# A fused two-layer ViT tower: strip copy and key masking moved from GpSimd to ScalarE, with new instruction orders on five engines

## The reference, cut to what matters

```python
h = patchify(x) @ W.T + b;  h = concat(cls_tok, h)          # 17 tokens x 192
h = h + topk_softmax_attention(layernorm(h))                # 12 heads of 64, 12 of 17 keys kept
h = h + ternary_gated_ffn(layernorm(h))                     # 8-bit activations, weights -1, 0, 1
h = h + linear_attention(layernorm(h))                      # below
h = h + norm_ffn(layernorm(h))                              # 192 -> 128 -> 192 -> layer norm

# in linear_attention, causal over the 17 tokens of an image:
q_f = elu(q) + 1;  k_f = elu(k) + 1                         # 12 heads of 16
params = silu(x @ Wb1) @ Wb2;  gate = f(tanh(params))
out = norm(sum_j (q_f.k_f[j]) * (1 + gate[j]) * v[j] / (sum_j q_f.k_f[j]))
```

## Time and profile before

| | |
|---|---|
| median of three runs | 668.53 us |
| profiled execution, its own time | 664.79 us |
| its span on the core | 662.9 us |
| PE busy | 577.5 us, 87% of the span |
| DVE busy | 501.5 us, 76% |
| POOL busy | 352.9 us, 53% |
| ACT busy | 254.9 us, 38% |

### The profile page before, as it was taken

One profiled execution on the slowest core, in us unless ns is written; L12 is line 12 of the kernel. 1 busy time (PEld: TensorE's weight loads), 2 busy tenths in 40 slices (PEclk: granted clock), 3 DMA queues, 4 the chain that ended last, 5 costly groups with the idle time before them and its releaser, 6 DMA issues.

```text
span 662.9 us, 15406 instructions
## 1 busy us (share of the span) xinstructions
PE 577.5 (87%) x5065; PEld 471.7 (71%) x5065; DVE 501.5 (76%) x2149; ACT 254.9 (38%) x659; POOL 352.9 (53%) x884
## 2 busy tenths in 40 slices
PE   4467889999999999999999999999999999787553
PEld 3255567878878787877878787787878878665441
DVE  0527558798898989889898988989898898875532
ACT  2014233544535354453535445353544535232210
POOL 2011023666666666666666666666666656555542
PEclk9679989999999999999999999999999999867575
DMA  9730010000100100010000000000000000000000
GB/s 212 162 81 1 1 43 22 2 22 1 28 19 11 28 1 28 3 26 13 13 26 0 26 0 26 13 13 26 0 6 0 7 2 8 6 1 7 0 7 7
DMA packets 11122, 14.92 MB, mean 23 GB/s; under 512 B 2161, under 2 KB 8658, under 8 KB 11078
## 3 DMA queue, kind: packets, MB, share of 16 engines
q1 hardware_dynamic: 8774, 12.69, 7.6%
q10 hardware_dynamic: 2304, 1.67, 0.9%
HBM read 12.68 MB, written 1.67 MB: 22 GB/s over the span
## 4 chain that ended last, share of the span: by engine, by line
PE 60%; DVE 23%; issue 4%; SPq 4%; ACT 3%; POOL 3%; DMA 1%; DVEq 0%; POOLq 0%; ACTq 0%
PE bank_embed L1210 8%; PE bank_att L1284 6%; PE bank_lin L1368 5%; PE bank_embed L1180 5%; PE bank_embed L1215 5%; DVE kept L718 5%; PE bank_att L1086 4%; PE bank_att L1274 4%; SPq L387 3%; DVE scores L698 3%; PE bank_lin L1384 3%; DVE top L710 2%; PE bank_att L1244 2%; PE bank_ffn L1086 2%; PE bank_lin L1086 2%
## 5 line engine op out<-in xcount | busy, mean ns | idle before, releaser
L1210 PE MATMUL bank_embed<-norm0T,w_qkv 128*128 128x119 f32 x456 | 59.4, 282 | 8.5 <-DMA g_out<-L_ffn_g_out 6.8
L1210 PEld LDWEIGHTS bank_embed<-norm0T,w_qkv 128*128 128x128 f32 x456 | 56.8, 197 | 11.2 <-issue 6.8
L483 POOL TENSOR_TENSOR rstd<-spread,minus_half 119x1 f32<-119x1 f32 (+1 forms) x95 | 57.3, 603 | 7.5
L482 POOL TENSOR_TENSOR spread<-moments,gain_eps 119x1 f32<-119x1 f32 x57 | 12.2, 214 | 85.2 <-DVE moments L673 85.1
L742 DVE TENSOR_TENSOR weightsT<-bank_lin,consts 119x476 f32<-119x476 f32 x57 | 36.8, 648 | 18.3 <-PE bank_lin L1368 18.3
L984 ACT COPY qkT<-bank_embed 128x357 f32<-128x357 f32 x76 | 30.9, 462 | 42.6 <-PE bank_embed L1215 42.6
L698 DVE TENSOR_REDUCE scores<-bank_att 119x51 f32<-119x357 f32 x76 | 37.6, 517 | 12.3 <-PE bank_att L1244 11.0
L1368 PE MATMUL bank_lin<-feat_qk,feat_k 32*119 32x119 f32 x456 | 42.5, 277 | 3.0 <-DVE weightsT L742 2.6
L483 POOL TENSOR_TENSOR rstd_h<-spread_h,minus_half 119x12 f32<-119x12 f32 x19 | 43.3, 2277 | 1.5
L950 ACT COPY att1T<-bank_lin 96x238 f32<-96x238 f32 x19 | 6.7, 353 | 94.2 <-PE bank_lin L1086 94.2
L1180 PE MATMUL bank_embed<-w_tok,patchT 128*119 128x192 f32 x228 | 42.3, 337 | 0.6 <-ACT patchT L960 0.6
(11 more groups left out here) (232 smaller groups left out, 1551.8 us busy)
## 6 DMA issues: line engine op xcount, KB each, us to landing
strips<-x SPq DMA_DIRECT2D x19, 336.0 KB
out<-result ACTq DMA_DIRECT2D x18, 89.2 KB
w_qkv<-L_attn_w_qkv SPq DMA_DIRECT2D x2, 576.0 KB, 8.4
w_in_raw<-L_ffn_w_in SPq DMA_DIRECT2D x1, 768.0 KB, 12.4
w_tok_raw<-L_tok_W SPq DMA_DIRECT2D x1, 576.0 KB
w_qkv_rest<-L_attn_w_qkv SPq DMA_DIRECT2D x2, 288.0 KB, 9.2
w_o<-L_attn_w_out SPq DMA_DIRECT2D x1, 576.0 KB
w_qkv_raw<-L_attn_Wqkv SPq DMA_DIRECT2D x1, 432.0 KB
```

The lines of the kernel that those rows point to most:

```text
L483: pool.tensor_tensor(rstd_out, spread, minus_half[0:ROWS, 0:spread.shape[1]], ALU.pow) \
L1210: pe.matmul(parts((E0, E1)[s], 3)[:, j], w_qkv0[:, tile * 128:(tile + 1) * 128], norm0T[:, s, :], start=j == 0, stop=False, skip_group_che ...
```

## The change

Two steps move from POOL to ACT. `p_strips` becomes `a_strips`, one ACT copy with the same patterns; a small padding operation of POOL that stood ahead of the copy is dropped. `p_feat_k` becomes `a_feat_k`, two ACT activations (Copy) with the 0/1 column as their per-partition scale. What waits for them, and for what they wait, is unchanged.

The order lists of POOL, DVE, ACT and PE are all rewritten. Some steps are also moved across the end of the iteration: `t_qk(0)` and `t_norm3` from the start of an iteration to the end of the one before, and so for `v_norm3`, `v_probs`, `v_hidT`, `p_rstd3`, `p_gate` and `a_tanh_par`; their stage number falls by one with it, so that they still work on the same group.

```diff
--- before.py
+++ after.py
@@ -483,14 +483,6 @@
                 pool.tensor_tensor(rstd_out, spread, minus_half[0:ROWS, 0:spread.shape[1]], ALU.pow) \
                     .then_inc(rstd_ready, 1)
 
-            def p_strips(g, p):
-
-                pool.wait_ge(strips_in[p], 16 * (g // 2 + 1) if isinstance(g, int) else 8 * (g - p) + 16)
-                after(pool, S["patches1"], g)
-                pool.tensor_tensor(pad_pool[:, :], pad_pool[:, :], ones[:, 0:1], ALU.mult)
-                pool.tensor_copy(patches[:, :, :].rearrange("p x (r c) -> p x r c", r=PATCH),
-                                 strips[:, p].rearrange("p r (x c) -> p x r c", x=GRID)).then_inc(S["strips_cut"], 1)
-
             def p_rstd0(g, p):
                 pool.wait_ge(S["moments0"], g + 1)
                 rstd(g, chain_of(pool, S["spread0"], 1), S["rstd0"], moments0[:, 1:2], spread0[:, :], rstd0[:, :], eps_ln)
@@ -521,14 +513,6 @@
                 pool.wait_ge(S["moments2"], g + 1)
                 norms_chain(g, pool.tensor_tensor(spread2[:, 0], moments2[:, 1:2].to_broadcast([ROWS, 2]), gain2, ALU.mult))
                 rstd(g, norms_chain, S["rstd2"], spread2[:, 0], spread2[:, 1], rstd2[:, :], eps2)
-
-            def p_feat_k(g, p):
-
-                pool.wait_ge(S["feat_k_all"], g + 1)
-                for odd in range(2):
-                    keep = consts[0:HALF, C_PARITY + odd:C_PARITY + odd + 1].unsqueeze(2).to_broadcast([HALF, 2, ROWS])
-                    last = pool.tensor_tensor(feat_k[:, odd], feat_qk[:, 2:4, :], keep, ALU.mult)
-                last.then_inc(S["feat_k"], 1)
 
             def p_gate(g, p):
 
@@ -571,8 +555,8 @@
                 rstd(g, last_chain, S["rstd4"], moments4[:, 1:2], spread4[:, :], rstd4[:, :], eps_ln)
 
             iterations(pool, lambda i, parity, active: in_turn(i, parity, active, [
-                (1, p_h0), (0, p_strips), (5, p_h3_beta), (5, p_rstd3), (4, p_feat_k), (4, p_gate), (3, p_scaled), (3, p_rms),
-                (5, p_rstd4), (4, p_centred_sq), (4, p_rstd_h), (3, p_rstd2), (0, p_rstd0), (2, p_rstd1),
+                (3, p_scaled), (3, p_rms), (5, p_h3_beta), (5, p_rstd4), (1, p_h0), (4, p_centred_sq), (4, p_rstd_h),
+                (3, p_rstd2), (0, p_rstd0), (4, p_rstd3), (2, p_rstd1), (3, p_gate),
             ]), setup)
 
 
@@ -900,12 +884,11 @@
                 ((S["a_done01"], S["a_masked0"], L1), (S["a_done01"], S["a_masked1"], L0), (S["a_done2"], S["a_masked2"], L1)))]
 
             iterations(dve, lambda i, parity, active: in_turn(i, parity, active, [
-                (5, v_norm3), (4, v_feat), (4, v_hidT), (3, v_big_in), (2, v_probs), (2, v_wide(0)), (2, v_wide(1)),
-                (5, v_stats4), (4, v_causal[0]), (2, v_wide(2)), (3, v_gated), (4, v_causal[1]), (4, v_causal[2]), (4, v_v1),
-                (3, v_big_out), (4, v_ratio), (5, v_result), (2, v_h1), (4, v_sq_sum), (2, v_u_in), (1, v_pack(1, A1)),
-                (3, v_h2), (3, v_stats2), (1, v_pack(0, A0)), (4, v_att1), (0, v_h0), (0, v_stats0), (3, v_norms2),
-                (1, v_pack(3, A1)), (1, v_pack(2, A0)), (0, v_norm0), (1, v_top), (4, v_h3), (1, v_drop), (4, v_stats3),
-                (1, v_mix),
+                (2, v_wide(0)), (4, v_feat), (2, v_wide(1)), (3, v_big_in), (2, v_wide(2)), (5, v_stats4), (4, v_causal[0]),
+                (4, v_causal[1]), (3, v_gated), (4, v_causal[2]), (4, v_v1), (3, v_big_out), (4, v_ratio), (2, v_h1),
+                (4, v_sq_sum), (2, v_u_in), (3, v_h2), (1, v_pack(0, A0)), (3, v_stats2), (1, v_pack(1, A1)), (4, v_att1),
+                (0, v_h0), (0, v_stats0), (3, v_norms2), (1, v_pack(3, A1)), (0, v_norm0), (1, v_pack(2, A0)), (5, v_result),
+                (1, v_top), (1, v_drop), (4, v_h3), (1, v_mix), (4, v_stats3), (1, v_probs), (4, v_norm3), (3, v_hidT),
             ]), setup)
 
 
@@ -950,6 +933,13 @@
                     act.copy(dst, src).then_inc(done_sem, 1)
                 return step
 
+
+            def a_strips(g, p):
+
+                act.wait_ge(strips_in[p], 16 * (g // 2 + 1) if isinstance(g, int) else 8 * (g - p) + 16)
+                after(act, S["patches1"], g)
+                act.copy(patches[:, :, :].rearrange("p x (r c) -> p x r c", r=PATCH),
+                         strips[:, p].rearrange("p r (x c) -> p x r c", x=GRID)).then_inc(S["strips_cut"], 1)
 
             def a_patchT(n, bank_tile, turned, done_sem):
 
@@ -1031,6 +1021,14 @@
                 act.activation(exp_qk[:, :, :], parts(L1, 4)[0:HALF], ACT.Exp)
                 act.activation(relu_qk[:, :, :], parts(L1, 4)[0:HALF], ACT.Relu).then_inc(S["relu_qk"], 1)
 
+            def a_feat_k(g, p):
+
+                act.wait_ge(S["feat_k_all"], g + 1)
+                for odd in range(2):
+                    last = act.activation(feat_k[:, odd], feat_qk[:, 2:4, :], ACT.Copy,
+                                          scale=consts[0:HALF, C_PARITY + odd:C_PARITY + odd + 1])
+                last.then_inc(S["feat_k"], 1)
+
             def a_tanh_hid(g, p):
                 act.wait_ge(S["hid"], g + 1)
                 act.activation(tanh_hid[:, :], L0[:, 0:ROWS], ACT.Tanh, scale=0.5)
@@ -1068,11 +1066,12 @@
                     act.dma_start(out[bass.ds(g * ROWS, ROWS), :], result[:, p]).then_inc(stored[p], 16)
 
             iterations(act, lambda i, parity, active: in_turn(i, parity, active, [
-                (4, a_tanh_par), (3, a_int_in), (5, a_hid1), (1, a_qk(0)), (3, a_in_T), (2, a_probsT[1]), (2, a_probsT[0]),
-                (3, a_tanh_gate), (1, a_qk(1)), (2, a_probsT[2]), (3, a_square), (4, a_interference), (4, a_num_T),
-                (2, a_att[0]), (0, a_patchT(0, E0, S["patches0"], S["patchT0"])), (2, a_att[1]), (3, a_int_out), (3, a_out_T),
-                (0, a_patchT(1, E1, S["patches1"], S["patchT1"])), (4, a_att1_T), (3, a_norms_T), (0, a_norm0T), (3, a_qk1),
-                (0, a_v(1)), (0, a_v(0)), (3, a_tanh_hid), (5, a_store), (4, a_norm3_T), (1, a_exp),
+                (4, a_feat_k), (5, a_hid1), (3, a_int_in), (2, a_probsT[0]), (3, a_in_T), (1, a_qk(0)), (2, a_probsT[2]),
+                (2, a_probsT[1]), (3, a_tanh_gate), (0, a_strips), (3, a_square), (4, a_interference), (1, a_qk(1)),
+                (2, a_att[0]), (4, a_num_T), (0, a_patchT(0, E0, S["patches0"], S["patchT0"])), (2, a_att[1]), (3, a_int_out),
+                (0, a_patchT(1, E1, S["patches1"], S["patchT1"])), (3, a_out_T), (4, a_att1_T), (3, a_norms_T), (0, a_norm0T),
+                (3, a_qk1), (0, a_v(1)), (0, a_v(0)), (1, a_exp), (3, a_tanh_hid), (4, a_norm3_T), (3, a_tanh_par),
+                (5, a_store),
             ]), setup)
 
             act.wait_ge(stored[0], 16 * ((GROUPS + 1) // 2))
@@ -1432,12 +1431,12 @@
                 pe.matmul(M1[0:ROWS, 0:EMBED], hid1T[:, :], w2o[:, :], start=True, stop=True).then_inc(S["out4"], 1)
 
             iterations(pe, lambda i, parity, active: in_turn(i, parity, active, [
-                (5, t_norm3), (1, t_qk(0)), (4, t_params), (5, t_hid1), (4, t_lin((0, 1), S["a_done01"])), (3, t_int_in),
-                (5, t_out4), (2, t_probs(0)), (2, t_probs(1)), (3, t_gate), (1, t_qk(1)), (2, t_probs(2)),
-                (4, t_lin((2,), S["a_done2"])), (2, t_att0(1)), (2, t_att0(0)), (4, t_num),
-                (0, t_patches(0, E0, S["k_copied0"], S["patches0"])), (4, t_num_turn), (2, t_proj0), (3, t_int_out),
-                (0, t_patches(1, E1, S["k_copied1"], S["patches1"])), (1, t_dots(0)), (3, t_down), (0, t_embed),
-                (1, t_dots(1)), (4, t_att1), (3, t_norms2), (4, t_proj1), (0, t_norm0), (3, t_qk1), (0, t_v), (3, t_hid),
+                (4, t_params), (2, t_probs(0)), (5, t_hid1), (4, t_lin((0, 1), S["a_done01"])), (5, t_out4), (3, t_int_in),
+                (2, t_probs(1)), (2, t_probs(2)), (3, t_gate), (1, t_qk(1)), (4, t_lin((2,), S["a_done2"])), (2, t_att0(1)),
+                (2, t_att0(0)), (4, t_num), (0, t_patches(0, E0, S["k_copied0"], S["patches0"])), (4, t_num_turn),
+                (2, t_proj0), (0, t_patches(1, E1, S["k_copied1"], S["patches1"])), (3, t_int_out), (1, t_dots(0)),
+                (3, t_down), (0, t_embed), (1, t_dots(1)), (4, t_att1), (3, t_norms2), (4, t_proj1), (0, t_norm0), (3, t_qk1),
+                (0, t_v), (3, t_hid), (0, t_qk(0)), (4, t_norm3),
             ]), setup)
 
 
```

## The result

The changed kernel takes 674.38 us (median of 8 runs, 669.69 to 676.06) against 668.50 for the kernel before in the same series (8 runs, 664.18 to 673.75). The ratio is 1.0105, 95% interval 1.0072 to 1.0138: slower by 1%. The profiled execution took 676.06, its span is 674.2.

What follows compares the result with a forecast made beforehand. PE was taken to bound the kernel. Filling -5.3, steady part +7.6 and draining 0 summed to +2.3 us on 668.53, giving 670.8 us; the range was 662 to 677.5.

Steps and rivals of the forecast that it cites:

- the steady part: Entries into iterations 5 to 19: +0.43 us per ordinary iteration, +0.72 at a branch, together +7.6 us.
- uncovered: At a loop branch, PE's own branch stands between `t_norm3` and `t_params` with nothing hiding it: +0.57 us.
- gain 0.20: PE's wait before `norm3` goes, as `t_norm3` stands behind `t_qk(0)`: 0.20 us gained in an ordinary iteration, 0.63 at a branch.
- The filling: Start of the kernel, through iteration 4: early `t_qk(0)` gains, later waits give some back; sum -5.3 us (-6.7 to -2.4).
- The first term: Filling: first group's `t_qk(0)` runs ahead of the setup wait, in PE's old gap; -5.0 us, taken as -4.2 for the clock.
- a wait of 0.86 goes twice: -1.7: Filling, iterations 2 and 3: `t_probs(2)` ahead of `t_qk(1)` removes a 0.86 us wait before the attention, -1.7 us in all.
- The draining: Last iterations, where PE waits for chains (hidT, the gate, the head norm): costed at 0, 1.5 us either way.
- the third: Rival: the filling gives nothing because DVE's setup or the next setup steps' DMAs set its end; 675 us, chance 0.14.
- The first: Rival, faster: the two new waits don't come about, the store not holding ACT up; 664.0 us, chance 0.30.
- The second: Rival, slower: ACT's queue becomes the path from `t_params` to `t_lin`, with a wait of 0.85; 677 us, chance 0.16.
- The fourth: Rival: the strips copy on ACT delays `a_square` by 0.3 us per iteration; 675 us, chance 0.04.
- The rule of the ports: POOL and DVE share a port pair, so 2.25 us less POOL per group could bring DVE's end of the iteration forward.

Runs made afterwards that it cites:

- the kernel without gaps: Changed kernel with DVE's h3 ahead of the drop step, ACT's store ahead of the copies of v, and `t_probs(1)` ahead of `t_lin`: ratio 0.9929 to before.
- the transposes together: Changed kernel with ACT's store ahead of the copies of v and DVE's h3 ahead of the drop step, `t_probs(1)` and `t_probs(2)` adjacent: ratio 0.9969 to before.
- the moves alone: Kernel before with its own order lists, only the key masking and the strips copy moved from POOL to ACT: 665.59 us, ratio 0.9965 to before.
- the kernel with the late order: Changed kernel with `t_qk(0)` of the first three groups put back behind the setup steps: ratio 1.0123 to before.
- store early: Changed kernel with the store's DMA issue on ACT ahead of the copies of v: 665.55 us, ratio 0.9987 to before.
- the orders alone: Changed kernel with its new order lists, but key masking and strips back on POOL: 690.39 us, ratio 1.0339 to before.

## Why the prediction was right or wrong

**The mechanism of the steady part was right: the places of the gaps and their sum. The conversion into time was wrong.** By its own terms the prediction gives for the 13 periods measured here (9 ordinary, 4 at a branch) gaps of 8.7 us before `t_lin`, 2.3 before `t_hid` and -4.3 before `norm3`, together +6.7. The rows say 9.0, 2.1 and -4.6: +6.5. Two errors inside cancel: the ordinary gap was 0.59 in the loop, not 0.45, since the store holds ACT up until 0.32 after its issue starts; that at the branch was 0.91, not 1.17, since PE's own branch, put at 0.57 "uncovered", shows no cost, while ACT's, put at 0.15, shows 0.32. Yet the steady part grew by 2.5 us, not 6.5: 4.0 us less. PE's start-to-start times in one ordinary iteration, 531.29 on in before and 536.64 on in after, show why: from `t_hid` to `t_num` without the gap PE takes 13.33 in before and 12.99 in after, for the same steps. The largest piece is at the end of `t_hid`, in before and in after:

```profile
547.28 0.60 PE L1338 MATMUL bank_lin<-norms2T,w_g 96*128 96x119 f32 x4
548.09 0.41 PE L1086 MATMUL bank_ffn<-consts,norm 119*96 119x119 f32 x2 [0.21 <-DVE norm L876]
```

```profile
552.83 0.60 PE L1337 MATMUL bank_lin<-norms2T,w_g 96*128 96x119 f32 x4
553.26 1.50 PE L1209 MATMUL bank_embed<-norm0T,w_qkv 128*128 128x119 f32 x12
```

Its last four matmuls take 0.81 - 0.21 = 0.60 net of the gap where `t_norm3` waited behind them, and 0.43 where `t_qk(0)` follows at once. **The failing step is "gain 0.20" for the norm3 wait: removing it gave back the gap and 0.17 more, the end of the last matmuls, which the next step now overlaps.** By "TensorE: Matmul & The Clock Gate" of the Trainium skill (section "Single matmul latency") a single bf16 matmul at the full clock takes about 0.166 us beyond its columns; the 0.17 of these float32 rows is of that size. Over 13 iterations the 0.17 makes 2.2 of the 4.0 us. The rest lies in smaller pieces of either sign, which the prediction took as unchanged. The new waits have such a price as well: without its gap of 0.14 it is 0.91 from the start of the matmuls ahead of `t_hid` to its own, against 0.83 in before, and for `t_lin` 0.69 against 0.59. All pieces together show in PE's busy time: cut from `t_num` to `t_num`, an ordinary iteration of the loop has 28.32 of 28.77 us in before (299.63 on) and 27.94 of 29.04 in after (303.30 on). The period of 28.57 us of the kernel without gaps against 28.58 of before without its gap, and 28.28 with the transposes together, shows that which step follows which is worth 0.3 us per iteration. Why the transposes pay 0.3 for being split stays open.

**Strips and masks.** 1.07 against 1.05 and 0.88 against 0.86 predicted. Both were worked out from neighbours of like shape, and with the moves alone the steady part shows no cost.

**The filling** was put at -5.3. The first term is right: over the eight profiles of after and its variants with the early `t_qk(0)` and both steps on ACT, `t_embed` of iteration 1 starts at 45.1 on average (43.6 to 46.6), over the three with the late one at 49.2 (47.7 to 50.0), 4.2 less. **The failing step is the second, "a wait of 0.86 goes twice: -1.7".** In iteration 3 that wait went, but `wide` (1.53) and `int_in` (0.99) came, with a lower clock, and iteration 3 became 3.5 us longer than in the kernel with the late order. At `t_num` of iteration 4 the same eight and three are at 128.7 (125.2 to 130.7) and 129.7 (125.8 to 132.2): -1, within their scatter.

**The draining** was put at 0, with 1.5 either way, by the waits alone. **That is the largest miss: +6 to +9 us. Of these 5.5 to 6.2 lie in the two iterations in which the clock was lower, and go when it is held; the rest was not tested.** The prediction had weighed the clock in the filling, for one step, and nowhere else.

**The sum**: 2.5 - 1 and 6 or more is 7.5 or more between profiles, where the medians are 5.9 apart (a profile is one execution, and the filling and draining scatter); the forecast was 7.6 - 5.3 + 0 = 2.3. That the range held is in part luck: the steady part was put 4 us too high, the filling 4 too low and the draining 6 to 9 too low. Of the rivals, the third (675) named the time, for its reason only in part: the filling gave little, but the setup was not what took it back. The first was right about the store: with its hold-up gone (store early) the wait is 0.22, where it had 0.2, and the ratio is 0.9987, not to be told from 1. The second, ACT's queue as the path, is where the wait is, but at 0.6 and not 0.85. The fourth did not come. The point forecast lay within 0.5% of before; slower, which had 0.37, is what came.

**The rule of the ports.** With POOL's copy and masks gone DVE's busy time in an iteration of the loop, ordinary and at a branch, is 25.57 and 25.64, against 25.31 and 25.40 in before with the same cuts: nothing was given back. In before they held up no long operation of DVE: the first mask started behind `feat_qk`, overlapped it by 0.23 us (316.76 to 316.99) and itself took 0.68, where the second took 0.58; and `h3`, beside which the copy ran, has only one of its inputs in SBUF. In the orders alone POOL and DVE held each other up. "SBUF — State Buffer" of the Trainium skill (section "SBUF: two separate sides") has the engine that starts first hold the port pair for its whole instruction, and the other blocked. The rows of the orders alone agree: `rstd` (329.05) ends 0.39 after the `wide` that had started before it (329.68), `wide` (330.23) 0.51 after the first mask (330.75), and the second mask (331.69) 0.43 after that `wide` (331.26), each 0.14 to 0.16 less than it takes alone (0.55, 0.65 and 0.58). So each waited for the other's end with all but its first 0.15 us. Such a wait is in after, too, which shows both cases:

```profile
321.61 0.65 DVE L736 TENSOR_TENSOR wide<-probs,consts 119x476 f32<-119x476 f32 x1
321.63 1.02 POOL L483 TENSOR_TENSOR rstd<-spread,minus_half 119x1 f32<-119x1 f32 x1
...
350.68 0.54 POOL L483 TENSOR_TENSOR rstd<-spread,minus_half 119x1 f32<-119x1 f32 x1
350.80 0.66 DVE L736 TENSOR_TENSOR wide<-probs,consts 119x476 f32<-119x476 f32 x1
```

Where `wide` starts first, `rstd` takes 1.02 in place of 0.54. Where `rstd`, one number per partition, starts first, `wide` is not held up, though they overlap by 0.42 us; there the measurement goes against "for its whole instruction".

## What to carry to other kernels

When PE is the bound, put DMA issues on the helper engine's queue where that engine waits anyway: one in front of a step that PE needs cost 0.4 us per iteration, where the moved work itself cost nothing. A gap in PE's timeline is not its price: removing one gave back up to 0.17 us more than its length, so check the period, not the gap. Where a pipeline drains, look at PE's granted clock as well as at the waits: here two iterations of the same matmuls took 5.5 to 6.2 us longer, mostly because the matmuls themselves were slower. Filling the waits with added matmuls gave that back in one kernel and nothing in another, so it has to be measured.

## What the runs showed of the hardware

- Added, useless matmuls made a stretch shorter: 54.56 us with 38 matmul instructions (13.3 us of PE) more, against 60.25 without.
- The same twelve 128x119 matmuls took 1.60 us (31.66) and 2.89 (38.08) in one profile of after, at the two levels of the clock; in the filling, executions of one kernel differ by 6.3 us (125.81 and 132.15).
- A loop's branch back showed on ACT (0.57 idle against 0.25), and not on PE, whose `t_params` followed `t_norm3` after 0.25 us in both.
- Each of the 19 added `pe.matmul` calls in fp32 appears as two records (38 in all), of 0.49 us on average; they overlap, and together keep PE busy for 13.3 us.
- A DMA issue of 0.28 us on ACT's queue held the next activation until 0.32 us after its start (323.06 to 323.38).
- In the orders alone, a VectorE and a GpSimd operation that both had two float32 inputs in SBUF ran one behind the other where they overlapped, but for the first 0.15 us of the later one; in after, a GpSimd operation of one number per partition (350.68) held up nothing when it started first.
